# Scores in two half-precision parts, two heads in the row halves of the array, and projections of a later batch in half-token units over three sections

## The chip, the cores and the metric
One core of one Trainium2 chip. The metric is the device time of one launch in microseconds (us). The core's engines are TensorE (PE, weight loads PEld), VectorE (DVE), ScalarE (ACT), GpSimd (POOL) and SyncE (SP, which issues DMAs here).

## The reference, cut to what matters
Sixteen waveforms become 750 tokens of 192 features each (framed DFT, mel energies, log, DCT, projection). Then:

```python
h = tok(x)                                  # (16, 750, 192)
a = layernorm(h)
q, k, v = a@V_Q@U_Q + b_q, a@V_K@U_K + b_k, a@V_V@U_V + b_v      # 12 heads of 16
s = (q_h @ M_U) @ (M_V @ k_h.T) / 4         # per head, 750 x 750
h = h + softmax(s) @ v_h
f = layernorm(h)                            # top-2 of 8 experts, plus a shared one
h = h + sum_e combine[t, e] * (swiglu((f@W1[e]+B1[e]) * (f@W3[e]+B3[e])) @ W2[e] + B2[e])
```

## The kernel before
**Stages.** Up to about 220 us the kernel makes the tokens of all batches and prepares weights. Then come 16 batches. A batch is three sections (four heads each; `att(b, g, tiles)`) with the feed-forward part (ffn) of the batch before between sections 1 and 2.

**A section** is an explicit list of tiles made by `schedule`. For each k of 0 to 23 there is an A tile and a B tile. Both are scores of 125 tokens against 750, in one PSUM slot (two banks, one per 375 tokens). Tile number p of the list uses slot p % 3, and TensorE waits (`slot_read`) until tile p-3 has been read.

- **A tiles** (`a_tile`) run eight ahead of the next section. Queries stand in the columns of the array; VectorE takes the row maxima (`amax`, L925). After 24 of them `max_parts` (L932 to L935) splits the maxima into three bf16 parts, TensorE turns them (`turn_maxima`, at k=18), `copy_mT` (L944) copies them, and SP writes them as three more rows under the stacked q (`load_maxrows`, L402).
- **B tiles** (`b_tile`) are the transposed scores minus the maximum, by these three rows. ScalarE takes exp (L746) of 750 elements into `probs`.
- **PV** (`pv`, four pieces for each key tile of 125): probabilities times values, fp32, four heads in the column quarters of the array (8 matmuls in the profile). One piece follows each A tile from k=6 on (two at k=6); the last four of a section follow A and B of k=0 and 1 of the next.
- After B of k=3 the outputs of the section before are turned (`turn_outputs`); VectorE normalises them at k=4 (L953, L956), POOL adds them to h (L496).

**Precision of scores.** q and k are split in three bf16 parts (`parts`), stored to DRAM and loaded back as stacks (`load_stacks`): six parts of 16 rows each (QPARTS, KPARTS), so 96 rows, and 99 with the maxima. One head's product is one 96-row matmul for each half of 375.

**P tiles** (`pre_tile`) make q, k, v of batch b+2, all nine in section 2, at the steps of PRE_AFTER: two turns of the normalised tokens, four tiles of q and k (8 fp32 matmuls each, for 750 tokens), three of v. For a q/k tile ScalarE copies PSUM to `rest` (L671; this frees the slot) and to the first part (L675), VectorE subtracts (L920), ScalarE copies the second part (L687), POOL subtracts for the third (L522).

**F tiles** (`prep_tile`) make ffn's input in section 0: two turns after k=14, side by side in the list, the gate's product after k=18, its turn after k=20. ScalarE copies each turned half to `xA`/`xB` (L695; frees the slot) and to half precision (L697); VectorE's `ffn_low` subtracts later. At k=5 to 8 VectorE makes ffn's statistics, at k=11 and 12 ScalarE applies them (`ffn_apply`, L709, L713).

**SP's queue** in a batch: load of h, maxima of section 1, stacks of the next batch's sections 0 and 1, stores of y, load for the norm, maxima of the next section 0, stores of parts and v, stacks of section 2.

Of the kernel before, what the change touches and what calls it, by code (L numbers as in the profile page):

```python
# [21 lines left out]
B, T = 16, 120000  # L22
# [8 lines left out]
HC = 375  # L31
# [20 lines left out]
NPRE, NPREP = 9, 4  # L52
PRE_AFTER = {2: (0, 1), 6: (2,), 8: (3,), 10: (4,), 12: (5,), 14: (6,), 16: (7,), 19: (8,)}
PRE_RESTS = {k + 1: tiles[0] - 2 for k, tiles in PRE_AFTER.items() if 2 <= tiles[0] < 6}
PREP_AFTER = {14: (0, 1), 18: (2,), 20: (3,)}


def schedule(prep=False, pre=None, a_tiles=TILES):
# [4 lines left out]
    for k in range(TILES):  # L63
        tiles.append(("A", k) if k < a_tiles else ("M", k) if k == MT_AT and a_tiles > 15 else None)
        tiles.append(("B", k))
        if prep:
            tiles += [("F", i) for i in PREP_AFTER.get(k, ())]
        if pre is not None:
            tiles += [("P", i, pre) for i in PRE_AFTER.get(k, ())]
# [3 lines left out]
def first_schedule():  # L73
# [27 lines left out]
def build(nc, x, melT, dct, w_proj, b_proj, vqT, uqh, vkT, uk, vvT, uv, bqh, bk, bv, muT, mv, gwT, gb,  # L101
# [4 lines left out]
    with ctx:  # L106
# [8 lines left out]
        qk_dram = nc.dram_tensor("qk_scratch", (B, 2, 3, E, NF), bf16, kind="Internal").ap()  # L115
# [4 lines left out]
        idb = sb("idb", [128, 128], bf16)  # L120
# [88 lines left out]
        wst = [qs[:].rearrange("p g c -> p (g c)").bitcast(fp32)[:, 2 * NFF * i:2 * NFF * i + 2 * NFF] for i in range(2)]  # L209
# [13 lines left out]
        sel_s = tmp(4 * NE1, CH * 128)  # L223
        assert o_ <= 4 * 3 * NF // 2
# [19 lines left out]
        raw_ready, rest_ready, part2_ready, parts_ready = sem("raw_ready"), sem("rest_ready"), sem("part2_ready"), sem("parts_ready")  # L244
# [8 lines left out]
        x2_turned, x2raw_ready, x2hi_ready, x2lo_ready = sem("x2_turned"), sem("x2raw_ready"), sem("x2hi_ready"), sem("x2lo_ready")  # L253
# [33 lines left out]
        def tile_read(tile, b, g):  # L287
# [8 lines left out]
            if kind == "F":  # L296
                return (x2raw_ready, 2 * (b - 1) + k + 1) if k < 2 else ((gate_copied, gate_read)[k - 2], b)
# [18 lines left out]
        def _(sp):  # L316
# [57 lines left out]
            def load_stacks(m, g):  # L374
# [1150 lines left out]
```

## Time and profile before

| what | value |
|---|---|
| median of 3 runs (lowest to highest) | 3370.38 us (3369.93 to 3396.47) |
| the profiled execution | 3367.23 us, span 3365.4 us |
| PE busy | 3107.8 us, 92% |
| DVE busy | 2156.2 us, 64% |
| ACT busy | 1673.6 us, 50% |
| POOL busy | 628.7 us, 19% |
| mean granted TensorE clock | 0.965 |
| maxima, exps | 1152 of 935 ns, 1152 of 794 ns |

Busy times of engines overlap. PE's are modelled: a matmul's record covers its passage through the array, so records of neighbours overlap, and a start-to-start distance says more of its pace than a duration. The granted clock is 1 at 2.4 GHz and 0.5 at 1.2 GHz.

### The profile page before, as it was taken

What the parts mean: (1) busy time and instruction counts of PE and PEld (TensorE: products, weight loads), DVE (VectorE), ACT (ScalarE), POOL (GpSimd) and SP (SyncE); (2) the same over time, 40 slices, a digit from 0 to 9 for tenths busy, and PEclk for the clock granted to TensorE, in tenths of its full rate; (3) what the DMA queues carried; (4) which work ended last, traced back from release to release, by engine and by line L of the source; (5) the groups of instructions that cost most, each with busy time, mean ns of one, the idle gap of its engine ahead of it and who ended that gap; (6) DMA issues with size and microseconds to landing.
All of it is one profiled execution on the core that took longest, in us unless ns stands there. A gap on an engine that the chain in (4) does not pass through costs nothing.

```text
span 3365.4 us, 56327 instructions
## 1 busy us (share of the span) xinstructions
PE 3107.8 (92%) x22512; PEld 1783.1 (53%) x22512; DVE 2156.2 (64%) x3860; ACT 1673.6 (50%) x2419; POOL 628.7 (19%) x1097
## 2 busy tenths in 40 slices
PE   6878999999999999999999999999999999899977
PEld 3544455464655546464554546455554646455545
DVE  3317666766767676666767676676667667667635
ACT  1133654646455464646455464645546464655542
POOL 1160120302112030301203030121203021120211
PEclk7667999999999999999999999999999999999989
DMA  5334320303122130312212031222203031221000
GB/s 136 103 102 99 79 45 15 90 23 79 23 71 39 32 80 15 80 23 71 38 53 59 14 80 29 72 34 63 46 15 89 22 79 23 64 38 30 5 8 8
DMA packets 146212, 174.52 MB, mean 52 GB/s; under 512 B 30081, under 2 KB 134874, under 8 KB 143950
## 3 DMA queue, kind: packets, MB, share of 16 engines
q1 hardware_dynamic: 143772, 163.37, 20.2%
q0 software_dynamic: 1280, 7.08, 0.9%
q8 instruction: 177, 2.90, 0.4%
q10 hardware_dynamic: 898, 0.47, 0.1%
q14 instruction: 85, 0.70, 0.1%
HBM read 105.49 MB, written 64.51 MB: 51 GB/s over the span
## 4 chain that ended last, share of the span: by engine, by line
PE 69%; DVE 13%; ACT 7%; issue 4%; POOL 3%; DMA 2%; SPq 2%; DVEq 0%; ACTq 0%; POOLq 0%
PE ps L1114 66%; DVE negm L925 7%; ACT big L746 3%; DVE st L873 2%; ACT hn L709 1%; DMA h_scratch<-h0t 1%; ACT rest L671 1%; PE ps L1286 1%; ACT parts L687 1%; PE ps L1198 1%; DVE mpart L932 1%; SPq L386 1%; DVE onrm L956 1%; DVE rest L1029 1%; POOL h0t L496 0%
## 5 line engine op out<-in xcount | busy, mean ns | idle before, releaser
L925 DVE TENSOR_REDUCE negm<-ps 125x1 f32<-125x750 f32 x1152 | 1064.1, 935 | 536.9 <-PE ps L1114 524.7
L746 ACT ACTIVATE big<-ps 125x750 f32<-125x750 f32 x1152 | 906.5, 794 | 651.8 <-PE ps L1114 648.7
L1114 PE MATMUL ps<-qs,ks 99*125 99x375 bf16 x2304 | 613.3, 348 | 66.6 <-DVE negm L925 58.0
L1114 PE MATMUL ps<-ks,qs 96*125 96x375 bf16 x2304 | 585.1, 336 | 62.8 <-ACT big L746 28.7
L1114 PE MATMUL ps<-big,V 125*32 125x188 f32 (+1 forms) x9216 | 584.6, 333 | 3.3 <-ACT big L746 0.4
L1029 DVE SCALAR_TENSOR_TENSOR rest<-ps,fb,h1s 128x375 f32<-128x375 f32 (+1 forms) x448 | 251.7, 603 | 322.7 <-PE ps L1114 321.6
L1114 PEld LDWEIGHTS ps<-qs,ks 99*125 99x125 bf16 x2304 | 228.8, 135 | 399.1 <-issue 221.9
L1114 PEld LDWEIGHTS ps<-ks,qs 96*125 96x125 bf16 x2304 | 290.8, 139 | 207.9 <-ACT big L746 52.6
L760 ACT ACTIVATE h1s<-ps,fb,wsc 128x375 f32<-128x375 f32 (+1 forms) x448 | 272.0, 657 | 210.3 <-PE ps L1114 210.3
L496 POOL TENSOR_TENSOR h0t<-h0t,onrm 125x384 f32<-125x384 f32 x48 | 48.0, 1001 | 1741.8 <-DVE onrm L956 1741.8
L1114 PEld LDWEIGHTS ps<-big,V 125*32 125x32 f32 x9216 | 195.8, 108 | 298.9 <-issue 285.1
L773 ACT ACTIVATE th<-xg 128x375 f32<-128x375 f32 (+1 forms) x224 | 115.5, 516 | 400.3 <-DVE xg L1033 400.3
L1114 PE MATMUL ps<-x2Ah,wAh 128*128 128x375 f16 (+1 forms) x896 | 290.1, 324 | 0.6 <-DVE lg L987 0.4
L1114 PE MATMUL ps<-x2Ah,wAl 128*128 128x375 f16 (+1 forms) x896 | 289.6, 323 | 0.0
L1114 PE MATMUL ps<-x2B,wBl 128*128 128x375 f16 (+1 forms) x896 | 289.6, 323 | 0.0
L1114 PE MATMUL ps<-x2B,wBh 128*128 128x375 f16 (+1 forms) x896 | 289.6, 323 | 0.0
L1114 PE MATMUL ps<-x2Al,wAh 128*128 128x375 f16 (+1 forms) x896 | 289.5, 323 | 0.0
L1114 PE MATMUL ps<-w2s,gg 128*125 128x192 f32 (+1 forms) x1344 | 273.6, 342 | 0.0
L1114 PEld LDWEIGHTS ps<-w2s,gg 128*125 128x125 f32 (+1 forms) x1344 | 211.8, 187 | 37.2 <-issue 37.2
L522 POOL TENSOR_TENSOR parts<-rest,parts 128x750 bf16<-128x750 f32 x64 | 98.0, 1533 | 321.4 <-ACT parts L687 321.4
L1041 DVE SCALAR_TENSOR_TENSOR rest<-th,xg 128x375 f32<-128x375 f32 (+1 forms) x224 | 120.9, 540 | 22.6 <-ACT th L773 22.2
L1051 DVE TENSOR_TENSOR gg<-ps,gt 128x375 f32<-128x375 f32 (+1 forms) x224 | 122.9, 549 | 16.3 <-PE ps L1114 9.2
(176 smaller groups left out, 3237.3 us busy)
## 6 DMA issues: line engine op xcount, KB each, us to landing
qs<-qk_scratch SPq DMA_DIRECT2D x288, 93.8 KB, 3.5
ks<-qk_scratch SPq DMA_DIRECT2D x288, 93.8 KB, 4.5
qk_scratch<-parts SPq DMA_DIRECT2D x32, 562.5 KB, 4.7
v_scratch<-vtmp SPq DMA_DIRECT2D x16, 1125.0 KB
V<-v_scratch SPq DMA_DIRECT2D x48, 375.0 KB
h_scratch<-h0t SPq DMA_DIRECT2D x16, 562.5 KB
hn<-h_scratch SPq DMA_DIRECT2D x16, 562.5 KB
h0t<-h_scratch SPq DMA_DIRECT2D x16, 562.5 KB
```

The lines of the kernel that those rows point to most:

```text
L386: sp.dma_start(qs[16 * s:16 * s + 16, g, :].rearrange("p (h t) -> p h t", h=HG), src).then_inc(stacks_loaded[g], 16)
L496: P_.tensor_tensor(v, v, onrm[:].rearrange("p (j h) d -> p j (h d)", j=J), op=ADD).then_inc(h_added, 1)
L522: P_.tensor_tensor(parts[0:rows, t, 2, :], rest[0:rows, t % 2, :], parts[0:rows, t, 1, :], op=SUB).then_inc(parts_ready, 1)
L746: nc.scalar.activation(halves(probs[:, i % 2, h, :]), slot(s, TP), ACT.Exp).then_inc(exp_done, 1)
L760: ins = nc.scalar.activation(h1s[0:rows, u % 2, s, :], ps[0:rows, s, 0:HC], ACT.Identity, bias=fb[0:rows, 2, s * CH + c:s * CH + c + 1], s ...
L773: nc.scalar.activation(th[0:rows, :], xg[0:rows, :], ACT.Tanh, scale=ALPHA / 2).then_inc(tanh_ready, 1)
L873: ins = V_.bn_stats(st[:, j, :], src[:, j, :])
L925: V_.tensor_reduce(negm[:, n:n + 1], slot(s, TP), axis=AX.XY, op=MAX, negate=True).then_inc(max_done, 1)
L1029: ins = V_.scalar_tensor_tensor(hh[0:rows, s, :], ps[0:rows, 2 + s, 0:HC], fb[0:rows, 3, s * CH + c:s * CH + c + 1], h1s[0:rows, u % 2, s, ...
L1041: chf.link(V_.scalar_tensor_tensor(ga[0:rows, :], th[0:rows, :], 1.0, xg[0:rows, :], op0=ADD, op1=MUL))
L1051: V_.tensor_tensor(gg[0:rows, u % 3, :], ps[0:rows, 4, 0:HC], gt[0:rows, u % 2, :], op=MUL).then_inc(g_ready, 1)
L1114: return nc.tensor.matmul(o, l, r, start=start, stop=stop)
```

## The change
1. q and k are split in two fp16 parts; three part pairs of 16 rows are stacked (48 rows, 50 with the maxima in two parts). The stacks hold two heads of four in rows 0 to 63 and two in rows 64 to 127. A tile is now two heads by 375 tokens: two matmuls, one in each row half, each into its own bank. The counts of tiles, of matmuls and of their columns stay.
2. q's and k's weights are scaled by powers of two; exp undoes this by a scale read from a column of SBUF. The maximum is two columns a tile; `max_parts` has three operations and not four.
3. P tiles are 13: two turns, eight q/k units of 375 tokens (4 matmuls each), three of v. They are spread over all three sections. ScalarE copies the unit from PSUM to the first part, and VectorE subtracts from PSUM to the second; the slot is free after that. POOL has no third part.
4. The two F turns stand apart (after k=13 and k=15), each with one copy on ScalarE and `ffn_low` on VectorE, which reads PSUM and frees the slot. `low` runs on VectorE at the next B tile of the list, after the A tile's maximum.
5. `pre_norm` is a batch further ahead (b+3), its VectorE part in section 2; the load for it stands earlier in SP's queue, stores of parts go one by one. Stacks are 12 DMAs of half the bytes, maxima four DMAs and not three.
6. In the setup, weights for ffn get buffers of their own, and products of weights run two a step.

```diff
-SLOTS = 6
-QPARTS = ((0, 3, 0), (3, 2, 1), (5, 1, 2))
-KPARTS = ((0, 3), (3, 2), (5, 1))
+QPARTS = (0, 0, 1)
+KPARTS = (0, 1, 0)
+SLOTS = len(QPARTS)
...
-NPRE, NPREP = 9, 4
-PRE_AFTER = {2: (0, 1), 6: (2,), 8: (3,), 10: (4,), 12: (5,), 14: (6,), 16: (7,), 19: (8,)}
...
-PREP_AFTER = {14: (0, 1), 18: (2,), 20: (3,)}
+NPRE, NPREP = 13, 4
+PRE_AFTER = (
+    {3: (0,), 5: (1,), 10: (2,)},
+    {2: (3,), 6: (4,), 10: (5,), 14: (6,), 18: (7,)},
+    {2: (8,), 5: (9,), 8: (10,), 12: (11,), 16: (12,)},
+)
+PREP_AFTER = {13: (0,), 15: (1,), 18: (2,), 20: (3,)}
...
-            return (raw_ready, 4 * m + k - 1) if k < 6 else (v_ready, 3 * m + k - 5)
...
+            return (parts_ready, 8 * m + k - 1) if k < 10 else (v_ready, 3 * m + k - 9)
...
             def a_tile(g, n, s):
 
-                h, j = n // J, n % J
+                c, j, n2 = n // (2 * J), n % (2 * J) // 2, n % 2
                 for q in range(2):
-                    ins = mm(slot(s, TP)[:, q, :], qs[0:KROWS, g, NF * h + TP * j:NF * h + TP * j + TP],
-                             ks[0:KROWS, g, NF * h + HC * q:NF * h + HC * q + HC])
+                    r = slice(64 * q, 64 * q + KROWS)
+                    ins = mm(slot(s, TP)[:, q, :], qs[r, g, NF * c + TP * j:NF * c + TP * j + TP],
+                             ks[r, g, NF * c + HC * n2:NF * c + HC * n2 + HC])
                 ins.then_inc(a_done, 1)
...
-                    nc.scalar.activation(halves(probs[:, i % 2, h, :]), slot(s, TP), ACT.Exp).then_inc(exp_done, 1)
+                    nc.scalar.activation(probs[:, i % 2, 2 * c:2 * c + 2, HC * n:HC * n + HC], slot(s, TP), ACT.Exp,
+                                         scale=wsc[0:TP, 21:22]).then_inc(exp_done, 1)
...
-            def pre_rest(m, t):
+            def pre_rest(m, h, s):
+                t, q = divmod(h, 2)
                 rows = 128 if t % 2 == 0 else E - 128
-                r_ = rest[0:rows, t % 2, :]
-                dve.wait_ge(part1_ready, 4 * m + t + 1)
-                V_.tensor_tensor(r_, r_, parts[0:rows, t, 0, :], op=SUB).then_inc(rest_ready, 1)
+                dve.wait_ge(part1_ready, 8 * m + h + 1)
+                hi, lo = (parts[0:rows, t, c, HC * q:HC * q + HC] for c in range(2))
+                V_.tensor_tensor(lo, ps[0:rows, 2 * s, 0:HC], hi, op=SUB).then_inc(parts_ready, 1)
...
-                V_.tensor_reduce(negm[:, n:n + 1], slot(s, TP), axis=AX.XY, op=MAX, negate=True).then_inc(max_done, 1)
+                V_.tensor_reduce(negp[:, 2 * n:2 * n + 2], slot(s, TP), axis=AX.X, op=MAX, negate=True).then_inc(max_done, 1)
...
-            def ffn_low(m, i):
+            def ffn_low(m, i, s):
...
-                    V_.tensor_tensor(x2Al[:], xA[:], x2Ah[:], op=SUB).then_inc(x2lo_ready, 1)
+                    V_.tensor_tensor(halves(x2Al[:]), slot(s), halves(x2Ah[:]), op=SUB).then_inc(x2lo_ready, 1)
...
+                        if low is not None:
+                            low()
+                            low = None
+                        if g == 2 and b + 3 < B and 6 <= k < 10:
+                            pre_norm(b + 3, k - 6)
+                    if kind == "F" and k < 2:
+                        def low(k=k, s=s):
+                            ffn_low(b - 1, k, s)
+                    if kind == "P" and 2 <= k < 10:
+                        def low(k=k, s=s):
+                            pre_rest(b + 2, k - 2, s)
```

## Rows read from the trace of the kernel before

**Rows 1.** Page, busy us of each engine.

```profile
PE 3107.8 (92%) x22512; PEld 1783.1 (53%) x22512; DVE 2156.2 (64%) x3860; ACT 1673.6 (50%) x2419; POOL 628.7 (19%) x1097
```

**Rows 2.** Windows: stretch, length, busy us (x count), PEclk, DMA; a batch.

```profile
1564.10:1604.70 40.60, 36.10 (x324) 18.09 (x325) 28.20 (x53) 26.31 (x38) 6.67 (x13) 1.00 0.29 86
1604.70:1637.40 32.70, 31.29 (x294) 16.12 (x294) 25.62 (x47) 19.68 (x25) 22.19 (x48) 1.00 0.26 46
1637.40:1704.10 66.70, 66.06 (x411) 43.51 (x410) 46.57 (x98) 26.07 (x45) 0.00 (x0) 1.00 0.15 27
1704.10:1758.60 54.50, 50.57 (x355) 28.65 (x353) 30.48 (x40) 30.69 (x41) 7.13 (x5) 0.97 0.17 50
```

**Rows 3.** Timeline: start, us, engine, operation; TensorE, plain steps, section 1.

```profile
1625.09 0.49 PE L1114 MATMUL ps<-ks,qs 96*125 96x375 bf16 x2
1625.51 0.52 PE L1114 MATMUL ps<-big,V 125*32 125x187 f32 x8
1625.96 0.54 PE L1114 MATMUL ps<-qs,ks 99*125 99x375 bf16 x2
1626.34 0.48 PE L1114 MATMUL ps<-ks,qs 96*125 96x375 bf16 x2
```

**Rows 4.** Timeline, VectorE and ScalarE, the same stretch.

```profile
1624.37 0.94 DVE L925 TENSOR_REDUCE negm<-ps 125x1 f32<-125x750 f32 x1 [0.30 <-PE ps L1114]
...
1626.54 0.80 ACT L746 ACTIVATE big<-ps 125x750 f32<-125x750 f32 x1 [0.45 <-PE ps L1114]
```

**Rows 5.** Lines by form: count | busy us, mean ns | idle before.

```profile
L649 ACT ACTIVATE big<-ps,lneps 40x750 f32<-40x750 f32 x16 | 14.1, 881 | 106.1 <-PE ps L1114 106.1
...
L1051 DVE TENSOR_TENSOR gg<-ps,gt 128x375 f32<-128x375 f32 x192 | 105.5, 549 | 6.6
...
L682 ACT ACTIVATE vtmp<-ps 125x384 f32<-125x384 f32 x48 | 23.3, 488 | 28.1 <-PE ps L1114 28.1
```

**Rows 6.** Timeline, TensorE, around a k projection in section 2.

```profile
1534.57 0.90 PE L1114 MATMUL ps<-xA,wk 128*128 128x375 f32 x2 [0.51 <-ACT big L746]
...
1537.20 0.49 PE L1114 MATMUL ps<-ks,qs 96*125 96x375 bf16 x2
...
1540.50 0.84 PE L1114 MATMUL ps<-xA,wk 128*64 128x375 f32 x2 [0.66 <-ACT big L746]
```

**Rows 7.** Timeline, TensorE, B tiles around the ffn input's turns, section 0.

```profile
1585.59 0.53 PE L1114 MATMUL ps<-qs,ks 99*125 99x375 bf16 x2
...
1590.16 0.54 PE L1114 MATMUL ps<-qs,ks 99*125 99x375 bf16 x2
```

**Rows 8.** Timeline, VectorE, splitting of maxima in section 2.

```profile
1549.29 1.52 DVE L932 CAST mpart<-negm 125x24 bf16<-125x24 f32 x1
...
1551.06 0.18 DVE L934 CAST mpart<-mres 125x24 bf16<-125x24 f32 x1
```

**Rows 9.** Windows: first A tiles; ffn_apply; the same place, last batch.

```profile
256.00:270.00 14.00, 14.00 (x34) 4.67 (x33) 14.00 (x17) 0.00 (x0) 0.00 (x0) 0.50 0.83 128
...
1583.20:1586.60 3.40, 2.30 (x20) 1.34 (x20) 1.37 (x2) 2.51 (x5) 0.00 (x0) 1.00 0.14 37
...
3106.40:3109.90 3.50, 2.02 (x19) 0.79 (x22) 1.04 (x2) 3.47 (x7) 0.00 (x0) 1.00 0.09 7
...
3109.90:3113.20 3.30, 3.30 (x21) 2.55 (x21) 0.94 (x1) 1.32 (x3) 0.00 (x0) 0.50 0.26 103
...
3113.40:3116.80 3.40, 3.10 (x28) 1.27 (x27) 2.57 (x7) 3.34 (x6) 0.00 (x0) 1.00 0.13 56
```

**Rows 10.** Timeline, TensorE, the stretch at 1.2 GHz.

```profile
3109.84 0.84 PE L1114 MATMUL ps<-big,V 125*32 125x187 f32 x8
...
3110.61 0.89 PE L1114 MATMUL ps<-qs,ks 99*125 99x375 bf16 x2
```

**Rows 11.** Timeline, POOL and TensorE, the start of attention.

```profile
216.40 1.51 POOL L522 TENSOR_TENSOR parts<-rest,parts 128x750 bf16<-128x750 f32 x1
...
286.71 0.86 PE L1114 MATMUL ps<-qs,ks 99*125 99x375 bf16 x2 [6.20 <-DMA qs<-mTs]
```

More of the change, by code:

```diff
@@ L68, in schedule @@
         if pre is not None:
-            tiles += [("P", i, pre) for i in PRE_AFTER.get(k, ())]
+            tiles += [("P", i, 2) for i in PRE_AFTER[pre].get(k, ())]
     return tiles + [None] * (-len(tiles) % 3)
@@ L76, in first_schedule @@
     tiles += [("P", i, 1) for i in range(NPRE)]
-    tiles += [("A", n - LEAD) for n in range(LEAD)] + [None]
-    assert len(tiles) % 3 == 0
-    return tiles
+    tiles += [("A", n - LEAD) for n in range(LEAD)]
+    return tiles + [None] * (-len(tiles) % 3)
 class Chain:
@@ L300, in tile_read, with sections @@
                 return (xA_ready, xB_ready)[k], m + 1
-            return (raw_ready, 4 * m + k - 1) if k < 6 else (v_ready, 3 * m + k - 5)
-        PLAIN, FIRST = schedule(), first_schedule()
-        SECTIONS = (schedule(prep=True), PLAIN, schedule(pre=2))
+            return (parts_ready, 8 * m + k - 1) if k < 10 else (v_ready, 3 * m + k - 9)
+        FIRST = first_schedule()
         LAST_A = 2 * TILES - LEAD
+        def sections(b):
+            pre = (0, 1, 2) if b + 2 < B else (None, None, None)
+            a_tiles = (TILES, LAST_A, 0) if b == B - 1 else (TILES, TILES, TILES)
+            return [schedule(g == 0 and b > 0, pre[g], a_tiles[g]) for g in range(G3)]
         def in_slot(tiles):
@@ L419, in body @@
                     load_stacks(b + 1, 1)
-                if do_ffn:
+                if b > 0:
                     store_y(b - 1)
-                if do_pre and more:
-                    load_hP(b + 3)
+                if do_pre:
+                    store_parts(b + 2)
                 if nxt:
@@ L442, in _ @@
             store_v(1)
-            body(0, do_ffn=False)
-            body(1)
-            for b in range(2, B - 3):
+            for b in range(B):
                 body(b)
-            body(B - 3, more=False)
-            body(B - 2, do_pre=False)
-            body(B - 1, do_pre=False, nxt=False)
             store_y(B - 1)
@@ L516, in pre_norm @@
                 ins.then_inc(ln1_ready, 1)
-            def third_parts(m):
-                for t in range(4):
-                    rows = 128 if t % 2 == 0 else E - 128
-                    pool.wait_ge(part2_ready, 4 * m + t + 1)
-                    P_.tensor_tensor(parts[0:rows, t, 2, :], rest[0:rows, t % 2, :], parts[0:rows, t, 1, :], op=SUB).then_inc(parts_ready, 1)
             def fold(dst, src, n):
```

314 lines of the change are left out of this document (152 added, 162 removed).

## The prediction

> **What bounds the kernel now.** I read the page first: TensorE is busy 92% of the span, VectorE 64%, ScalarE 50% [rows 1]. One batch by stages [rows 2] gives the weights: section 0 takes 40.6 us, section 1 32.7, the feed-forward part (ffn) 66.7, section 2 54.5. The change leaves ffn alone, so it can only move the 127.8 us of the sections.
>
> Then the timeline of a plain stretch. One step k of a section is one A tile, one piece of the value product (PV), one B tile, and A follows A after 1.25 us (1625.09, 1626.34) [rows 3]. Of that, A to PV is 0.42, PV to B 0.45, B to A 0.38. The reader is to see that no wait stands in these rows: this is TensorE's own pace, with two matmuls of 0.16 us in each tile and a switch of about 0.09 when the form of the tile changes. VectorE needs 0.94 for the maximum and ScalarE 0.80 for the exp of the same step [rows 4], so both have slack. Of the 24 steps of a section 17 have one PV, k=6 has two, k=0 and 1 have two of the section before, and k=2 to 5 have none; those four already wait for the maxima.
>
> **Step 1, the pairs.** A and B each become two matmuls on 48 or 50 rows, one in each half of the array, into different banks. If they run side by side, a tile costs one stream (0.16) and not two. TensorE's own step is then 1.25 - 0.32 = 0.93. But a new wait ends last. Three slots of PSUM go round, so A of step k+2 needs the exp of B of step k. B's weights to exp's start was 0.58 (1625.96, 1626.54), with one matmul of the pair gone 0.42 [rows 3, 4]. The exp gets its scale from a column of SBUF: without such a column it took 0.80 [rows 4], and the one ACTIVATE of 750 elements that reads a column (the Ln's bias) 881 ns [rows 5], so I take 0.80 + 0.09 = 0.89. Then 0.05 to release, 0.05 + 0.25 for A up to PV, 0.45 for PV: 0.42 + 0.89 + 0.05 + 0.30 + 0.45 = 2.1 us for two steps, 1.05 a step. Gain 0.19 x 17 = 3.2; at k=0, 1 and 6 TensorE's own 0.9; at k=2 to 5 none. That is -4.1 a section, -12.4 a batch. Bounds: 0.93 a step (exp hidden) gives -18; 1.25 (pairs one after the other) gives 0.
>
> No row shows two matmuls in row halves; the PV rows show four on column quarters in 0.53 us [rows 3]. The Trainium skill, "TensorE: Matmul & The Clock Gate", Part 3, says that row tiles run concurrently and measured 3.07 times for four; by it the pair costs one stream, which is what I take.
>
> **Step 2, less cover.** Copies of outputs, the normalisation and the splitting of maxima sat in slack of 0.3 to 0.45 a step [rows 4]; now 0.1 to 0.15 is left. Three inserts of 0.8 to 1.0 a section lose some 0.2 each more: +0.6 a section, +1.8 a batch (bounds 0 and 4).
>
> **Step 3, projections of q and k.** Before, a full tile costs 2.63 of TensorE (1534.57 to 1537.20) and the two steps around it take 5.93 [rows 6]: 5.93 - 2 x 1.25 = 3.4, times 4 = 13.7 a batch. Behind that stood the ScalarE chain of three copies (two are left out now) and POOL's third part.
> After, eight units. Count from B's start: unit 0.25 to 1.55 (half of 2.63), switch, next A at 1.70, its maximum 2.07 to 3.01. Only then comes the unit's low part on VectorE, which is queued behind that maximum: 0.55 by the 375-wide rows from PSUM [rows 5]. The slot is free at 3.6, because it is now read twice, by ScalarE (0.49 [rows 5], done at 2.2) and by VectorE. A of two steps on starts at 3.65, its B at 4.4. Without the unit it would be 2.1, so a unit costs 2.3, and 8 cost 18.4: +4.7. Lower bound: 1.3 each (TensorE only), -3; upper 2.8, +9. The three V units and two turns cost what they did; where they stand doesn't matter. The unit's DMAs halve in bytes; the queue of SP has 12 loads a stack as before.
>
> **Step 4, the ffn input.** The two turns (F tiles) go in separately, each with its low part read from PSUM. By the same count A two steps on waits until 3.4 and each costs 2.1, together 4.2. Before, both cost 4.57 - 2 x 1.25 = 2.1 (1585.59 to 1590.16) [rows 7]: +2.1. The norm's own work beside them (six ACTIVATEs, statistics) has less cover: +0.8. One wide copy each (0.83) falls away on ScalarE, behind the same wait.
>
> **Step 5, POOL.** The third parts leave POOL. While they ran, a cast of 24 columns on VectorE took 1.52 us, and the next of the same size 0.18 [rows 8]: -1.2 a batch.
>
> **Step 6, start and end.** POOL could begin the first third part only at 216.40, and the first B tile waited until 286.71 for its rows of maxima [rows 11], behind three groups of stacks on SP. Now parts need no POOL and stacks are half as large, but batch 1's projections still wait for POOL's norm, which ends at 216.4, and the first A tiles stand behind them: about -10 (0 to -25).
>
> Sum at full clock: -12.4 + 1.8 + 4.7 + 2.9 - 1.2 = -4.2 for each of 13 middle batches, -55; batch 0 (no ffn input) -7; batch 14 (no projections) -8; batch 15 -6; start -10. In all -86, from the profiled run's 3367 (span 3365.4; 3 below the median of 3370): 3281.
>
> **Step 7, the clock.** TensorE does the same work in less streaming time and waits more. Where ScalarE normalises for ffn (a stretch like 1583.2) TensorE was busy 2.30 of 3.4 us and stayed at 2.4 GHz; in the last batch the same place had 2.02 of 3.5 and the next stretch ran at 1.2 [rows 9]. After the change each A or B there streams half as long, with the same waits, so I expect a fall here in nearly every batch, and at some starts of sections. At 1.2 GHz PV takes 0.77 and a pair of matmuls 0.68, so 0.34 for one [rows 10]: a step becomes 0.34 + 0.34 + 0.1 + 0.77 = 1.55, +0.5. Eight steps and two longer units or turns a batch: +5, for 15 batches +75. Forecast: 3281 + 75 = 3356; I say 3355, that is 15 below the median.
>
> A rule against this step: the Trainium skill, same page, "Why this matters for your kernels", asks only that long idle gaps be avoided for full clock. By that rule no batch would lose it and the time would be 3281 (rival 1). The trace doesn't bear it out: the clock fell after TensorE had been busy more than half of the stretch.
>
> **Rivals.**
> Rival 1, the clock holds. For it: in the batch shown the ffn place stayed at 2.4 GHz [rows 9], and a pair may keep the clock up like the two matmuls it replaces. Against: the fall of the last batch. Time 3281, own range 3220 to 3330.
> Rival 2, slower: once low, the clock stays low to the end of a section. For it: in 256 to 270, A tiles only, TensorE worked all the time and the clock stayed at 1.2 GHz [rows 9]; a plain step at 1.2 leaves TensorE streaming even less than all the time. Against: in the last batch it was back in the stretch from 3113.4 [rows 9], and ffn's dense matmuls should bring it back in each batch. A low section costs 17 x 0.5 + 4 units x 1.2 = 13; one more section in most batches adds 125 to 195: 3480 to 3550, I take 3490. It decides as soon as more than 2 of each 3 falls last a section.
> Rival 3, the pairs don't run side by side: step 1 gives nothing, the rest stays: +1.8 + 4.7 + 2.9 - 1.2 = +8 a batch, x 13, ends about -5: 3465. For it: no row shows a row pair. Against: the column quarters do run so [rows 3].
> Rival 4, rows of maxima come late: they are written from k=18 on and due at k=0, so 6 steps of 1.05 for 6 of 1.25 are left, and it is four small DMAs and not three. Against: but for the start [rows 11], no B tile of the page's groups waited long for them. If they are 1 us late each time, 48 sections give +48: 3400.
>
> **Numbers.** Forecast 34%, rival 1 28%, rival 2 28%, rival 3 7%, rival 4 3%. The forecast's own range is 3320 to 3400. For 8 in 10 the range takes rival 1 down to 3260 and rival 2 up to 3520. Faster by over 1% (under 3337; 1% is about what a measurement of this kernel can tell): rival 1 and a quarter of the forecast, 0.36; slower by over 1% (over 3404): rivals 2 and 3 and some of 4, 0.37; within 1%: 0.27.
>
> **What the profile after will show.** Step 1: A to PV about 0.30 us, a plain step at 1.05, with a wait of A for the exp; exp at 0.88. If the step is 1.25, rival 3. Step 3: between two B tiles around a unit 4.4 us, A waiting for VectorE's low part. Step 4: such a wait of 0.8 to 1.3 us after each turn. Step 5: all casts of maxima under 0.5. Step 7: stretches at 1.2 GHz in section 0 of most batches, mean clock 0.88 to 0.94 (0.965 before); above 0.96 speaks for rival 1, under 0.85 for rival 2. Wrong would be, above all, a cost of 1.3 for a unit (other work fills the wait), or a clock that follows something else than waits.

## The result, and the profile after

The changed kernel takes 3454.15 us (median of 4 runs, 3444.21 to 3486.62): 1.024 of the kernel before, 95% interval 1.016 to 1.032. The time lies inside the range said for 8 in 10 (3260 to 3520), outside the forecast's own (3320 to 3400), and on the other side of no change: 80 us more and not 15 less. The profiled execution has a span of 3442.3 us against 3365.4. The medians and ratios of this document leave out single runs in a slower state that every kernel falls into at times, and one disturbed run of e11 (5397 us).

The page of the changed kernel: busy us, the granted clock in 40 slices (tenths), the exp.

```profile
PE 3093.6 (90%) x22512; PEld 1593.6 (46%) x22512; DVE 2131.6 (62%) x3889; ACT 1676.9 (49%) x2323; POOL 531.7 (15%) x1033
...
PEclk7867889798998989898998979899897989886789
...
L726 ACT ACTIVATE big<-ps,wsc 125x750 f32<-125x750 f32 x1152 | 1014.6, 887 | 704.1 <-PE ps L1112 696.0
```

TensorE is busy 14 us less than before [rows 1], though each tile of scores streams half as long: much of it now runs at the lower clock, where it takes twice the time. A batch by stages, section 0, section 1, ffn, section 2 (stretch, length, busy us of PE, PEld, DVE, ACT, POOL, clock, DMA):

```profile
1573.80:1619.90 46.10, 39.42 (x339) 17.35 (x339) 28.38 (x52) 28.93 (x39) 5.61 (x11) 0.81 0.21 67
1620.00:1665.80 45.80, 40.98 (x317) 15.49 (x316) 26.08 (x36) 24.26 (x30) 15.75 (x43) 0.79 0.08 22
1665.80:1733.60 67.80, 67.03 (x415) 43.79 (x413) 45.95 (x97) 26.10 (x45) 0.00 (x0) 0.99 0.07 19
1733.60:1772.00 38.40, 34.30 (x319) 17.11 (x318) 28.44 (x53) 23.67 (x29) 8.49 (x9) 1.00 0.16 47
```

Against [rows 2], section 2 is 16 us shorter, since three quarters of its q and k projections moved away, but sections 0 and 1 are 5.5 and 13 longer, at a mean clock of 0.8. The same batch, cut where the clock changes:

```profile
1595.20:1612.30 17.10, 14.82 (x82) 6.29 (x83) 7.16 (x11) 7.72 (x10) 0.00 (x0) 0.50 0.10 36
1612.30:1629.30 17.00, 14.78 (x153) 6.76 (x155) 11.55 (x18) 11.62 (x15) 9.87 (x29) 1.00 0.29 80
1629.30:1632.70 3.40, 3.40 (x22) 1.21 (x13) 1.29 (x2) 0.98 (x2) 3.16 (x4) 0.50 0.19 57
1632.70:1649.80 17.10, 14.12 (x136) 5.30 (x135) 11.18 (x16) 9.51 (x13) 4.65 (x17) 1.00 0.00 1
1649.80:1666.90 17.10, 16.89 (x103) 5.75 (x102) 7.23 (x10) 7.50 (x9) 0.00 (x0) 0.50 0.04 10
```

So 37.6 of 198.0 us run at 1.2 GHz, in every one of the 13 middle batches at the same three places. Where the 77 us between the spans arose (changed kernel first, then the kernel before; cut at the first exp of batches 0, 1, 14 and 15):

```profile
0.00:271.40 271.40, 195.95 (x687) 109.34 (x687) 114.52 (x211) 44.46 (x62) 73.95 (x65) 0.76 0.41 113
271.40:387.10 115.70, 105.56 (x927) 44.73 (x929) 76.16 (x114) 72.02 (x88) 9.47 (x10) 0.86 0.17 52
387.10:2960.40 2573.30, 2360.86 (x17905) 1216.59 (x17905) 1670.57 (x3053) 1338.47 (x1860) 381.94 (x798) 0.91 0.12 36
2960.40:3155.20 194.80, 184.13 (x1313) 87.60 (x1310) 123.31 (x213) 96.12 (x130) 22.47 (x54) 0.75 0.09 27
3155.20:3442.30 287.10, 247.12 (x1694) 135.39 (x1694) 147.01 (x299) 125.79 (x186) 43.82 (x106) 0.82 0.03 10
```

```profile
0.00:287.60 287.60, 221.28 (x686) 123.42 (x687) 109.06 (x176) 55.01 (x69) 79.04 (x65) 0.68 0.46 117
287.60:401.30 113.70, 108.45 (x927) 56.56 (x929) 77.88 (x112) 70.06 (x91) 15.60 (x14) 0.99 0.27 64
401.30:2916.20 2514.90, 2378.63 (x17905) 1369.33 (x17909) 1699.22 (x3056) 1334.43 (x1937) 467.90 (x858) 1.00 0.21 49
2916.20:3089.30 173.10, 165.48 (x1313) 94.94 (x1317) 123.50 (x216) 91.19 (x133) 22.41 (x54) 1.00 0.18 42
3089.30:3365.40 276.10, 233.97 (x1694) 138.85 (x1687) 146.51 (x301) 122.86 (x190) 43.79 (x106) 0.93 0.06 12
```

Start -16, batch 0 +2, the 13 middle batches +58 (4.5 each), batch 14 +22, the rest +11. The clock is lower in each stretch from the first exp on.

**The steps at full clock.** Two plain steps in section 2 (timeline: start, us, engine, operation):

```profile
1767.62 0.33 PE L1112 MATMUL ps<-ks,qs 48*125 48x375 f16 x2
...
1767.88 0.53 PE L1112 MATMUL ps<-big,V 125*32 125x188 f32 x8
...
1768.33 0.37 PE L1112 MATMUL ps<-qs,ks 50*125 50x375 f16 x2
1768.76 0.13 PEld L1112 LDWEIGHTS ps<-ks,qs 48*125 48x125 f16 x2 [0.30 <-ACT big L726]
...
1769.73 0.33 PE L1112 MATMUL ps<-ks,qs 48*125 48x375 f16 x2
```

From A to the A two steps on it is 2.11 us, every second A waits for an exp, and exp takes 0.89. That is step 1 of the prediction to the hundredth. A step of the same kind at 1.2 GHz, in section 1:

```profile
1659.61 0.52 PE L1112 MATMUL ps<-ks,qs 48*125 48x375 f16 x2
...
1661.21 0.52 PE L1112 MATMUL ps<-ks,qs 48*125 48x375 f16 x2
```

One step is 1.60 there (forecast 1.55). A unit in section 1, on TensorE and then on VectorE:

```profile
1638.11 0.84 PE L1112 MATMUL ps<-xA,wq 128*64 128x375 f32 x2
...
1641.38 0.37 PE L1112 MATMUL ps<-ks,qs 48*125 48x375 f16 x2 [0.72 <-DVE parts L912]
...
1639.94 0.94 DVE L917 TENSOR_REDUCE negp<-ps 125x2 f32<-125x750 f32 x1 [1.53 <-PE ps L1112]
1640.79 0.53 DVE L912 TENSOR_TENSOR parts<-ps,parts 64x375 f16<-64x375 f32 x1
```

The second A behind it waits for the low part, which stands behind a maximum, as step 3 had it. And the wait in front of the first fall (ScalarE, then TensorE; the last row is the kernel before at the same work):

```profile
1593.37 1.41 ACT L691 ACTIVATE hn<-h0t,nmr,rstd 125x192 f32<-125x192 f32 x3
...
1595.24 1.65 ACT L726 ACTIVATE big<-ps,wsc 125x750 f32<-125x750 f32 x2
...
1596.16 1.51 PE L1198 MATMUL ps<-idf,hn 125*128 125x125 f32 x6 [1.45 <-ACT big L726]
...
1584.67 0.54 PE L1114 MATMUL ps<-ks,qs 96*125 96x375 bf16 x2 [1.10 <-ACT big L746]
```

ScalarE normalises for ffn ahead of the exps, and TensorE stands 1.45 us from 1594.71 on; at 1595.20 the clock falls. The kernel before stands 1.10 us at the same work and keeps its clock. The two stretches are hardly different in busy time: 2.18 of 3.40 us (1591.80 to 1595.20) against the 2.30 of [rows 9]. So the wait was there already, and it alone doesn't say why the clock falls now.

### The profile page after: what moved, and what is told of

It reads as the page before. It is cut to its first block, busy times and chain, and to the rows that moved or that the text cites. A ratio compares the mean times of both kernels' runs of the same rounds, so it can differ in the third digit from the quotient of the medians.

```text
span 3442.3 us, 56178 instructions
## 1 busy us (share of the span) xinstructions
PE 3093.6 (90%) x22512; PEld 1593.6 (46%) x22512; DVE 2131.6 (62%) x3889; ACT 1676.9 (49%) x2323; POOL 531.7 (15%) x1033
## 4 chain that ended last, share of the span: by engine, by line
PE 73%; DVE 14%; ACT 7%; issue 2%; DMA 2%; POOL 1%; SPq 1%; DVEq 0%; ACTq 0%; POOLq 0%
PE ps L1112 69%; DVE negp L917 8%; ACT big L726 6%; PE ps L1198 2%; DVE parts L912 1%; ACT hn L691 1%; DVE st L862 1%; SPq L398 1%; DMA hn<-h_scratch 1%; DMA h_scratch<-h0t 1%; DVE rest L1028 1%; PE ps L1287 1%; DVE x2B L975 0%; POOL h0t L502 0%; PE ps L1150 0%
## 5 line engine op out<-in xcount | busy, mean ns | idle before, releaser
L917 DVE TENSOR_REDUCE negp<-ps 125x2 f32<-125x750 f32 x1152 | 1061.7, 935 | 626.1 <-PE ps L1112 624.9
L726 ACT ACTIVATE big<-ps,wsc 125x750 f32<-125x750 f32 x1152 | 1014.6, 887 | 704.1 <-PE ps L1112 696.0
L1112 PE MATMUL ps<-big,V 125*32 125x188 f32 (+1 forms) x9216 | 678.3, 380 | 10.4 <-issue 5.8
L1112 PE MATMUL ps<-ks,qs 48*125 48x375 f16 x2304 | 463.0, 399 | 155.7 <-DVE parts L912 72.1
L1112 PE MATMUL ps<-qs,ks 50*125 50x375 f16 x2304 | 478.5, 413 | 60.9 <-DVE negp L917 57.0
L1112 PEld LDWEIGHTS ps<-qs,ks 50*125 50x125 f16 x2304 | 165.4, 140 | 446.8 <-issue 251.7
L1112 PEld LDWEIGHTS ps<-ks,qs 48*125 48x125 f16 x2304 | 170.1, 144 | 398.3 <-issue 112.2
L1112 PEld LDWEIGHTS ps<-big,V 125*32 125x32 f32 x9216 | 207.6, 116 | 276.5 <-issue 252.1
L1041 DVE SCALAR_TENSOR_TENSOR gt<-rest 128x375 f32<-128x375 f32 (+1 forms) x224 | 123.3, 551 | 7.7
```

The lines of the kernel that those rows point to most:

```text
L726: nc.scalar.activation(probs[:, i % 2, 2 * c:2 * c + 2, HC * n:HC * n + HC], slot(s, TP), ACT.Exp, scale=wsc[0:TP, 21:22]).then_inc(exp_do ...
L917: V_.tensor_reduce(negp[:, 2 * n:2 * n + 2], slot(s, TP), axis=AX.X, op=MAX, negate=True).then_inc(max_done, 1)
L1041: chf.link(V_.scalar_tensor_tensor(gt[0:rows, u % 2, :], xl[0:rows, :], 1.0, ga[0:rows, :], op0=ADD, op1=MUL))
L1112: return nc.tensor.matmul(o, l, r, start=start, stop=stop)
```

## The experiments

| run | median us | ratio to the kernel before, interval | clock of the profiled run | a middle batch, us |
|---|---|---|---|---|
| changed kernel | 3454 | 1.024 (1.016 to 1.032) | 0.876 | 198.0 |
| e1 fillers | 3522 | 1.045 (1.043 to 1.047) | 0.943 | 200 to 205 |
| e2 pair in one half, 48 rows | 4623 | 1.372 (1.368 to 1.375) | 0.660 | 276.5 |
| e3 constant scale | 3462 | 1.027 (1.024 to 1.030) | 0.860 | 201.4 |
| e4 low part first | 3433 | 1.018 (1.012 to 1.025) | 0.856 | 191 to 206 |
| e5 62 and 64 rows | 3412 | 1.013 (1.011 to 1.016) | 0.885 | 195 to 201 |
| e6 = e4 and e5 | 3281 | 0.975 (0.970 to 0.979) | 0.919 | 184 to 191 |
| e7 pair in series, 128 rows | 3377 (1 run) | | 0.972 | 194.6 |
| e8 section 1 without units | 3736 | 1.108 (1.102 to 1.114) | 0.779 | 216 to 219 |
| e9 F tiles later | 3477 | 1.035 (1.028 to 1.041) | 0.870 | 198.0 |
| e10 = e6 and e9 | 3216 | 0.956 (0.950 to 0.963) | 0.934 | 182 to 191 |
| e11 = e10, units moved | 3242 | 0.962 (0.957 to 0.967) | | |
| e12 before, 48 rows | 4497 (1 run) | | 0.665 | 266 to 270 |
| e13 ScalarE's normalisation spread | 3590 | 1.062 (1.059 to 1.065) | 0.818 | 194 to 224 |
| e14 = e6 and e13 | 3175 | 0.941 (0.939 to 0.942) | 0.963 | 180 to 183 |
| e15 = e14, units moved | 3191 | 0.945 (0.944 to 0.947) | 0.960 | 181 to 185 |
| e16 = e14 without e5 | 3311 | 0.984 (0.978 to 0.991) | 0.903 | 180 to 202 |
| e17 before, spread so | 3483 | 1.035 (1.030 to 1.040) | 0.937 | 201.4 |

**e1: fill the waits.** In TensorE's `att`, ahead of `slot_read`:

```diff
+            def filler(n, bank, start):
+                for _ in range(n):
+                    mm(ps[0:128, bank, 384:512], idf[:], idf[:], start, start)
...
+                    fill_wait(tiles, p, s)
```

> The changed kernel with fillers: fp32 matmuls of 128 columns (identity by identity) into 128 columns of PSUM that nobody reads, put on TensorE just before it waits for a slot: 6 before an A tile whose slot holds a P or F tile, 3 before such a B tile, 10 before the first F turn. The real work is the same. Theory 1 (what the change lost is TensorE's clock, and the clock falls because TensorE streams too little there): the stretches at 1.2 GHz of sections 0 and 1 go, section 0 takes about 40 us and section 1 about 38 and not 44 and 44, the batch 189 and not 198, the kernel 3320 to 3350. Rival (the low clock is not what costs, the waits for the units are): the batch stays at 198 or grows by the fillers, 3450 to 3480, whatever the clock shows.

Section 1 of it, and one filler stretch:

```profile
2084.40:2126.40 42.00, 40.59 (x380) 20.90 (x379) 26.05 (x36) 24.24 (x30) 14.56 (x40) 1.00 0.09 24
```

```profile
2006.06 1.60 PE L1112 MATMUL ps<-idf 128*128 128x128 f32 x12
```

In section 1 the clock came back (1.00, and 3.8 us shorter than 45.8), and in section 0 of a middle batch at most 3.4 us are low and not 17.1. But the fillers were wrongly sized: six instructions are twelve records, 0.11 us apart, and take 1.3 to 1.6 us where most waits were 0.7, and in section 2 most stood where nothing waited. There the clock, which held in the changed kernel, now fell for 6.8 us at the start in 12 of the 13 middle batches, and the section took 45.4 us from its first exp to its last, not 36.4. Neither theory's time came (3522 us); that more work in the waits keeps the clock up in section 1, and in most of section 0, is shown.

**e2, e7, e12: rows of the array.** e2 puts both matmuls into one half (`r = slice(0, KROWS)`), e7 runs both on 128 rows, e12 is the kernel before on 48 and 50 of its 96 and 99. (Exp has a constant scale in e7 and e12, so that it stays finite; the values that stream are thus not the real ones, but e7 and e12 share this and came out on opposite sides.)

```diff
-                    r = slice(64 * q, 64 * q + KROWS)
+                    r = slice(0, 128)
```

> The changed kernel with both matmuls of every A and B tile on rows 0 to 63 of the array (the second pair of heads is computed from the first pair's rows, so these scores are the wrong heads'). Everything else stays. Theory (row halves run side by side in the changed kernel): each tile now takes 0.16 more of TensorE, a plain step 1.25 and not 1.055, three sections of 17 such steps +10 us a batch at full clock; but TensorE streams more, so that most stretches at 1.2 GHz go, -9: the kernel 3430 to 3520, mean clock over 0.93. Rival (the pairs already run one after the other): A to the next group, the step and the time stay as they are, 3454.

> The counterpart of e2_onehalf: both matmuls of every A and B tile one after the other, but each on all 128 rows and not on 48 or 50 (the scores are sums over two heads, and exp is at a scale of 1e-15 of the right size so that it stays finite). Same instructions, same columns, same sequence. Theory 2: the clock is back near 0.95, a plain step 1.25 us, the kernel 3430 to 3520 and not 4623. Theory 1, or if e2's low clock had to do with its sequence: as e2, 4600.

> The kernel before, with its own schedule and its six bf16 parts, but A tiles on 48 rows and B tiles on 50 of its 96 and 99 (scores without half of their terms and without the maximum; exp at a scale of 0.001 so that it stays finite). Same instructions, columns and order. Theory 2 (the use of the array sets the clock): long stretches at 1.2 GHz, mean clock under 0.80, 3900 to 4600. Rival (e2's low clock came from the changed kernel's schedule): clock 0.96, 3360 to 3385.

Section 1 in a window each: e2, e7, e12, the kernel before.

```profile
2196.50:2266.50 70.00, 69.44 (x308) 26.94 (x308) 25.40 (x36) 24.40 (x30) 12.58 (x33) 0.50 0.05 13
```

```profile
1606.40:1648.90 42.50, 38.60 (x318) 18.28 (x311) 26.09 (x36) 24.26 (x30) 15.07 (x42) 1.00 0.09 23
```

```profile
2128.50:2182.60 54.10, 54.10 (x291) 23.34 (x288) 25.55 (x47) 19.90 (x25) 20.77 (x43) 0.50 0.16 25
```

```profile
1604.20:1636.80 32.60, 31.19 (x298) 15.95 (x295) 26.12 (x47) 19.68 (x25) 22.54 (x50) 1.00 0.26 48
```

e2 was expected at 3430 to 3520 and took 4623: with TensorE busy for 69.4 of 70 us the clock is 0.50. e7 has the same instructions in the same order on 128 rows, and in none of its middle batches does the clock fall; the kernel takes 3377 (one run). e12 shows it without anything of the change: half the rows, the instructions and order of the kernel before, 4497 (one run) and not 3363. In e12 the clock even falls without a wait, in section 0 of batch 7:

```profile
2116.50:2123.30 6.80, 6.80 (x61) 3.47 (x60) 3.99 (x7) 3.54 (x6) 0.00 (x0) 1.00 0.02 3
2123.30:2126.70 3.40, 3.40 (x22) 1.06 (x20) 1.29 (x2) 1.50 (x3) 2.83 (x8) 0.50 0.00 0
```

TensorE is busy for all of the 6.80 us before the fall. This falsifies what step 7 rested on (waits and less streaming bring the clock down) as the whole cause: the same stream of matmuls kept 2.4 GHz on 96 or 128 rows and lost it on 48. The page "TensorE: Matmul & The Clock Gate" of the Trainium skill says of the clock, in "Why this matters for your kernels", that gaps of idle time are to be avoided; these stretches of e2 and e12 have none and are at 1.2 GHz, so the measurement decides against it as a sufficient rule.

e7 also prices the pair: its plain section 1 (batch 14, no units) against that of e8, both at full clock:

```profile
2966.80:2998.40 31.60, 30.75 (x298) 15.24 (x291) 23.64 (x31) 21.85 (x25) 15.07 (x42) 1.00 0.12 31
```

```profile
1578.50:1606.50 28.00, 25.98 (x300) 11.19 (x299) 23.32 (x31) 21.74 (x25) 15.69 (x43) 1.00 0.15 36
```

3.6 us a section: the halves do run side by side (rival 3 is out). It also shows what the change would be without the lower clock: a batch of e7 takes 194.6 us, all at 2.4 GHz, less 3 x 3.6 for the pairs is 183.8 (an estimate), where the changed kernel takes 198.0.

**e5: 14 rows of zeros.** The maxima move to rows 62 and 63, rows 48 to 61 of the q stack are zero.

```diff
+MAT = 62
...
+            V_.memset(qs[:].rearrange("p g c -> p (g c)"), 0.0)
...
-                    r = slice(64 * q, 64 * q + KROWS)
+                    r = slice(64 * q, 64 * q + MAT)
...
-                    r = slice(64 * q, 64 * q + KROWS + MROWS)
+                    r = slice(64 * q, 64 * q + MAT + MROWS)
```

> The changed kernel with A tiles on 62 and B tiles on 64 rows of each half instead of 48 and 50: rows 48 to 61 of the q stack are zero and the maxima stand in rows 62 and 63, so the scores are exactly the same, and so are the number, columns and order of all instructions. The pair in one half (e2_onehalf) had TensorE busy nearly all the time and yet the lowest clock, with 48 rows in use where the kernel before has 96 in the same sequence. Theory 2 (the clock follows how much of the array is in use, not how long TensorE streams): more rows at the same timing hold the clock longer, the stretches at 1.2 GHz of 17 us get rarer, the kernel 3330 to 3420, mean clock 0.90 to 0.96. Theory 1 (it follows the share of time in which TensorE streams): nothing changes, 3440 to 3465, clock 0.87.

42 us less than the changed kernel, at the upper edge of theory 2's time and below its clock (0.885 to 0.899, not 0.90). In five of 13 middle batches section 1 keeps the clock, with the same instructions as the changed kernel's 45.8:

```profile
843.00:882.00 39.00, 33.53 (x320) 13.94 (x319) 26.04 (x36) 24.26 (x30) 15.78 (x43) 1.00 0.10 26
```

So the clock's price in section 1 is 6.8 us, and a unit costs (39.0 - 28.0) / 5 = 2.2 us. But the rows don't help everywhere: section 2, where the changed kernel's clock held, now has 13.7 us at 1.2 GHz in each of the 13 middle batches and takes 4 us longer. Where in a batch the clock falls thus shifts with the timing, and none of these runs says by what rule.

**e4 and e6: the low part ahead of the maximum.**

```diff
                     if kind == "A":
+                        if low is not None:
+                            low()
+                            low = None
                         amax(72 * b + 24 * g + k + LEAD, s, (k + LEAD) % TILES)
...
-                        if low is not None:
-                            low()
-                            low = None
```

> The changed kernel with the low part of a unit or turn ahead of the next A tile's maximum on VectorE, not behind it. Theory (a unit costs 2.2 us because its slot waits for the low part behind a maximum of 0.94): the slot is free 0.8 us sooner, a unit or turn costs 1.5 to 1.7, ten of them in a batch -6 us, and with shorter waits the clock may hold longer: 3330 to 3390. Rival (VectorE then stands waiting for ScalarE's copy and the maximum behind it is as late as before): 3440 to 3480.

> Both e5_rows64's rows and e4_lowfirst's order of VectorE. e4 took section 1 from 43.8 to 34.2 us where the clock held, and lost it in section 2 of some batches. Theory 2: with 62 and 64 rows the clock holds in most of those too, a batch is 180 to 188, the kernel 3240 to 3330. Theory 1: as e4_lowfirst, 3410 to 3460.

e4's section 1, at full clock in all middle batches but one, and its section 2 as it is in five of the 13:

```profile
1630.50:1666.70 36.20, 34.14 (x320) 13.93 (x319) 25.28 (x36) 24.22 (x30) 15.73 (x43) 1.00 0.11 28
...
1924.90:1980.90 56.00, 53.82 (x310) 23.70 (x309) 28.40 (x51) 23.63 (x29) 8.48 (x9) 0.55 0.13 40
```

A unit is (36.2 - 28.0) / 5 = 1.6 us now, as expected, but the time is the rival's: a section 2 that stays low eats it. With e5's rows as well no section 2 stays low (falls of 13.7 us at its start remain in 11 of 13 batches): 3281, 173 us under the changed kernel, where the two edits alone give 42 and some 20, the latter not clear of noise.

**e3: exp's scale as a constant.** `scale=wsc[0:TP, 21:22]` becomes `scale=2.0 ** -12`.

> The changed kernel with exp's scale as a constant in the instruction (2^-12) and not read from a column of SBUF; the softmax is at a wrong scale. Theory (the plain step is set by the chain slot, exp, slot, so exp's longer time counts): exp 0.80 and not 0.89 us, two plain steps 2.02 and not 2.11, about -2 us a batch, the kernel 3415 to 3430. Rival (the step is set elsewhere): exp shorter, step and time unchanged, 3454.

```profile
3076.57 0.37 PE L1113 MATMUL ps<-ks,qs 48*125 48x375 f16 x2
...
3078.59 0.37 PE L1113 MATMUL ps<-ks,qs 48*125 48x375 f16 x2
```

exp is 0.80 (797 ns), two plain steps are 2.02 us at full clock: the chain of step 1 is right. The kernel was expected at 3415 to 3430 and isn't faster, since 51.3 us of each middle batch are now at 1.2 GHz and not 37.6, 13.7 of them in section 2.

**e8: no units in section 1.** PRE_AFTER of section 1 is empty; ten P tiles, seven of them units, stand in section 2.

> The changed kernel with the five q and k units of section 1 moved to section 2 (after k = 1, 3, 5, 7, 9, then the others after 11, 13, 15, 17, 19). If units' waits bring the clock down, section 1 is 26 us as in batch 14 of e1_fill, and section 2, with ten units, 47 at full clock or 52 to 57 with falls: the batch 190 to 196 and not 198, the kernel 3370 to 3430. Rival (the units cost the same anywhere and the clock falls in section 1 without them too): section 1 over 30 us, batch 198 or more, 3454 or more.

Section 1 is 28.0 (above), without a fall. Section 2 was expected at 47 to 57 and is this:

```profile
1673.30:1746.50 73.20, 67.47 (x332) 28.80 (x330) 31.14 (x56) 26.10 (x34) 8.48 (x9) 0.57 0.10 32
```

Once low, the clock stays low for 68 to 82 us in the middle batches, past the end of the section and 9 to 14 us into the next section 0: rival 2's mechanism. The kernel took 3736 us, expected 3370 to 3430. With the units spread over three sections the change came out 280 us better than with them crowded into two.

**e9, e13, e17: what starts the fall in section 0.**

```diff
-PREP_AFTER = {13: (0,), 15: (1,), 18: (2,), 20: (3,)}
+PREP_AFTER = {14: (0,), 16: (1,), 19: (2,), 21: (3,)}     # e9
...
+PREP_AFTER = {16: (0,), 18: (1,), 20: (2,), 21: (3,)}     # e13
...
-PREP_AFTER = {14: (0, 1), 18: (2,), 20: (3,)}
+PREP_AFTER = {16: (0, 1), 20: (2,), 21: (3,)}             # e17
...
-                        if k in (11, 12):
-                            ffn_apply(b - 1, k - 11)
+                        if 10 <= k < 16:
+                            ffn_apply(b - 1, k - 10)      # e13, e17: one ACTIVATE a step
```

> The changed kernel with the F tiles one or two steps later: after k = 14, 16, 19 and 21, not 13, 15, 18 and 20. In every run so far TensorE stands 1.5 us before the first F turn, which waits for ScalarE's normalisation, and the clock falls right there. Theory (the change put the turn ahead of its input, and this wait alone makes the fall in section 0): the wait is under 0.6 us, section 0 is 39 to 41 and not 44.1, the batch 193 to 195, the kernel 3390 to 3415. Rival (the fall there comes with the low use of the array in general): section 0 shorter by the wait of about 1 us at most, 3435 to 3455.

> The changed kernel with ScalarE's normalisation for ffn one ACTIVATE at each of k = 10 to 15 (before: three at k = 11 and three and a copy at k = 12, ahead of these steps' exp), and the F tiles after k = 16, 18, 20 and 21. e9 moved only the F tiles, and the wait of 1.5 us moved to an A tile that waits for exp. Theory (the wait is ScalarE's 1.3 us of normalisation ahead of an exp, and it is what starts the fall of section 0): no single wait there is over 0.7 us, section 0 is 39 to 42 and not 44.1, batch 193 to 196, the kernel 3380 to 3430. Rival (the same 2.5 us of ScalarE's work cost as much spread out, and the fall comes anyway): 3445 to 3480.

> The kernel before with ScalarE's normalisation spread over k = 10 to 15 and its F tiles after k = 16, 20 and 21. It has slack of 0.45 us a step on ScalarE and a clock of 0.965. If the spreading is worth something by itself, it is the wait of 0.5 to 1 us in section 0 and the odd fall of 3.4 us: 3345 to 3365; if it is worth something only beside the shorter steps: 3365 to 3375. Either way it says how much of e14's gain is this edit's.

e9 moved the wait, not the fall:

```profile
1624.12 0.57 PE L1112 MATMUL ps<-ks,qs 48*125 48x375 f16 x2 [1.45 <-ACT big L726]
```

So the 1.45 us are ScalarE's normalisation ahead of an exp, wherever the turn stands, and the time (3477) met neither expectation. e13 takes that wait away, and the largest of section 0 is then this, for the low part of the first turn:

```profile
1706.37 0.32 PE L1266 MATMUL ps<-idh,mpart 125*72 125x125 f16 x1 [1.12 <-DVE x2Al L973]
```

At 1706.40 the clock falls there, for 10.2 us and not 17.1. The kernel is slower all the same: section 2, an unchanged program, now stays low in seven of the 13 middle batches:

```profile
994.50:1051.00 56.50, 54.45 (x312) 24.04 (x310) 28.61 (x52) 23.73 (x29) 8.50 (x9) 0.55 0.13 40
```

The same section 2 is 38.40 us at full clock (second fence of the result): a whole section at 1.2 GHz costs 18. Why section 2 changed isn't settled.

e17 was expected between 3345 and 3375 and took 3483, with 10.2 or 13.7 us at 1.2 GHz in section 0 of every batch but the first. It is no clean trial of the spreading. Its turns moved behind k=16, but VectorE's low parts stayed at k=15 and 16; VectorE stands there 2.98 us for ScalarE's copy of the turn, the maximum of an A tile waits behind it, and TensorE's second turn behind that:

```profile
1636.98 1.51 PE L1198 MATMUL ps<-idf,hn 125*128 125x125 f32 x6 [3.57 <-DVE negm L925]
```

Within this wait, at 1635.9, the clock falls, on 96 and 99 rows.

**e14, e16, e10, e11, e15: together.**

> e6_rows64_low with that spreading. Theory: section 0 keeps full clock and is 37 to 39 and not 43.4, the start of section 2 falls in some batches as in e10: batch 181 to 185, the kernel 3150 to 3210. Rival: as e10, 3210 to 3260.

> e14_spread without its rows: A tiles on 48 rows and B tiles on 50 as in the changed kernel, the low part first and ScalarE's normalisation spread. Theory (both the rows in use and the waits count, neither is enough): the clock is low for 40 to 80 us a batch, the batch 190 to 205, the kernel 3350 to 3550. Rival (the order on VectorE and ScalarE alone brings the clock back, the zero rows only add a little): 3175 to 3230.

> e6_rows64_low with the F tiles later as in e9_later. e6's profile shows two falls in most batches, before the first F turn and at the start of section 2. Theory: the first goes, section 0 is 37 to 39 and not 43.4, the batch 185 and not 191, the kernel 3190 to 3230. Rival: another wait of section 0 (the B tiles behind the P turns) brings the clock down all the same: 3260 to 3285.

> e10 with the units of section 2 at k = 6, 9, 12, 15 and 18 (not 2, 5, 8, 12, 16), so that none stands among the steps that wait for the maxima, and the unit of section 0 at k = 8, not 10. Theory: section 2 stays at full clock, 36 us and not 40.8 in all batches, and section 0 has a gap less before the F turns: batch 180, the kernel 3130 to 3190. Rival: the fall at the start of section 2 comes from its first steps, whatever stands among them: as e10.

> e14 with the units of section 2 at k = 6, 9, 12, 15 and 18 as in e11, whose profile fell into a disturbed execution and told nothing of section 2. Theory (a unit among the steps that wait for maxima brings the clock down at the start of section 2): section 2 is 36 us in every batch, the kernel 20 to 40 us below e14. Rival: the same as e14 within 15 us, with section 2 at 38 to 41 in some batches.

e14 by stages (section 0, section 1, section 2):

```profile
1465.50:1505.00 39.50, 33.47 (x339) 15.29 (x339) 27.97 (x52) 28.69 (x39) 5.50 (x11) 1.00 0.24 77
1505.10:1541.30 36.20, 34.13 (x320) 13.92 (x319) 25.28 (x36) 24.22 (x30) 15.87 (x43) 1.00 0.11 28
...
1608.10:1646.10 38.00, 34.57 (x316) 17.20 (x318) 28.31 (x53) 23.63 (x29) 8.49 (x9) 1.00 0.16 47
```

All hold 2.4 GHz (in three of the 13 middle batches section 2 has 6.8 us low); the kernel takes 3175 us, 5.9% less than the kernel before, and computes what the changed kernel does. e16 is the same without the zero rows: in four of 13 batches section 2 is low (56.5 us again), and in seven part of section 0 is; 3311 us in all, between what its theory (3350 to 3550) and its rival (3175 to 3230) said. The rows are worth about 140 us there, and neither they nor the order of the work is enough alone. The spreading cost 136 us by itself (e13), and gained 123 on e4 (e16) and 106 on e6 (e14). e10 met its 3190 to 3230, but not by its theory: falls of 3.4 to 17.1 us stayed in section 0 of all 13 middle batches. e11 was expected at 3130 to 3190 and took 3234 to 3249. e15 was expected 20 to 40 us below e14 and is 15 above: moving the units within section 2 gains nothing.

## Why the prediction was wrong, point by point

- **Step 1 (pairs): right.** 2.11 us for two steps, exp 0.89, A waiting for exp. A plain section 1 went from 32.6 to 28.0, 4.6 less; steps 1 and 2 together said 3.5.
- **Step 2 (less cover): too high.** That section holds the copies, the normalisation and the splitting, and gained more than step 1 alone said (4.1), so no loss is left to see.
- **Step 3 (units): right.** 2.2 us against 2.3, by the mechanism named, and 1.6 when the low part goes first.
- **Step 4 (ffn input): open in size.** The wait for ScalarE's normalisation grew from 1.10 to 1.45 us, within the 0.8 counted for less cover. The waits behind the turns are 0.60 and 0.72 (0.8 to 1.3 said), at 1.2 GHz. The turns' own price at full clock wasn't isolated.
- **Step 5 (POOL): right** where it can be read: the splitting's operations take 0.18 to 0.21 us now, none 1.5.
- **Step 6 (start): not shown.** The first exp came 16 us sooner in the profiled run (-10 said), but the kernels of e1 to e10 and e13 to e16, whose start is all but the same, have it at 277 to 293 us, and the kernel before at 288. So much of the 16 is chance.
- **Step 7 (clock): the step that failed.** The place was half right (a fall in section 0 of each batch), the price of a step at 1.2 GHz right (1.60 against 1.55), the mean clock just under the range (0.876, 0.88 to 0.94 said). Wrong were the length (eight steps and two units or turns, where 37.6 us of each batch are low, in two sections) and the batches without units: batch 14 (counted from 0) was put at -8, -3 with the clock, and is +22. At full clock a batch would be about 198.0 - 6.8 (section 1, e5) - 5.5 (an estimate for section 0: from A at 1597.61 to A at 1612.63 five steps, a turn and the gate's product, 5 x 1.055 + 2.1 + 1.6 + 0.5 = 9.5 at full clock, and 15.0 measured) - 1 (ffn's start) = 185, and e7 gave 184 by another way. The forecast without the clock was 189 (193.5 before, less 4.2): the sum of steps 1 to 6 was 4 to 5 us a batch too high, and the clock's 5 should have been 13. The first error helped by luck: with it mended the forecast would stand some 60 us lower, further from 3454.
- **The reason given in step 7** was that TensorE waits more. That is half of it: fillers in the waits keep the clock in section 1 (e1), and the same rows with shorter waits do so in more places (e6 against e5, e14 against e6). The other half no step had. The change halved the rows of each matmul of the scores, and by e2, e7 and e12 the same stream of matmuls on 48 rows runs at 1.2 GHz without any wait. Those three run a pair one after the other; that rows count in the changed kernel too, where the halves run side by side, is shown by e5, and by e16 against e14. The prediction named this as a sign of being wrong: a clock that follows something else than waits.
- **Rivals.** Rival 1's clock came true only with three more edits (e14: 3175). Rival 2's time (3490) was nearest; its rule, low to the end of a section, holds in e8, e13 and e4, and in the changed kernel for section 2 of batch 14 but not in its middle batches; its price for a low section, 13 us, is 18. It was left at 28%, because in the last batch of the kernel before the clock was back after 3.3 us. Rival 3 is out by e7. Rival 4 is out: in the whole trace nothing waits for the maxima's load.

## What to carry to other kernels

When a change makes matmuls narrower or runs them side by side on fewer rows, price it at both clocks, and take the clock as part of the result: the instructions saved here were worth 8 to 9 us a batch and the clock took 13. Rows of zeros cost no time here (a plain section 1 at full clock takes 26.0 us from first exp to last on 48 rows, e16, and on 62, e14) and were worth 42 us by themselves and about 140 beside two other edits. A wait is only half a reason for a fall: waits of 1.10 us on 96 rows and of up to 1.24 on 128 (e7) left the clock up, one of 1.45 on 48 came with a fall. So work on another engine that delays TensorE is to be spread or reordered, and then measured, because the same spreading cost 136 us in one kernel and gained 106 in another.

## What the runs showed of the hardware

- TensorE busy 96% of the span at a mean clock of 0.66 on 48 and 50 rows (e2), against 0.97 for the same instructions on 128 rows (e7); busy 97% at 0.665 (e12), against 0.965 on 96 and 99 rows (the kernel before).
- The clock can fall with no wait before it: e12, busy 6.80 of 6.80 us, then 1.2 GHz.
- Rows that hold zeros count: e5's zeros change no result and no other instruction, and with them the clock goes from 0.903 (e16) to 0.963 (e14).
- A section 2 at 1.2 GHz costs 56.5 and not 38.4 us, and the clock came back only 8 to 14 us into the next section 0 (e13, e16).
- An fp32 matmul of 128 columns shows as two records, 0.11 us apart, at 2.4 GHz (e1).
- A scale read from SBUF costs ScalarE 0.09 us for 750 elements (0.887 against 0.797 us, e3).
